# A pre-norm transformer layer on one core: GpSimd derives the norms' negated mean and variance plus epsilon, in place of VectorE

## What is computed

```python
x = x + attn(layernorm(x))     # 16 heads of 16, causal, window of 64 keys
x = x + ffn(layernorm(x))      # 256 -> 1024 -> 256, relu, ternary weights, biases

def layernorm(x, eps=1e-05):
    m = mean(x, axis=-1, keepdims=True)
    v = var(x, axis=-1, keepdims=True)
    return (x - m) / sqrt(v + eps)
```

## Time and profile before

| | before |
|---|---|
| median of the runs, us | 671.52 (667.95 to 671.65, 3 runs) |
| the profiled execution, us | 669.85 |
| its span, first to last instruction, us | 668.1 |
| mean granted TensorE clock | 0.992 |
| busy: PE, DVE, ACT, POOL, us | 645.6, 610.4, 565.0, 562.2 |
| instructions: PE, DVE, ACT, POOL | 8049, 1389, 2483, 837 |

### The profile page before, as it was taken

The page is one execution under the profiler, slowest core; times in us unless marked ns, Lnnn a source line. Parts: engine busy times, 40 slices in busy tenths (PEclk is TensorE's granted clock), DMA queues, the critical chain, the costliest instruction groups (busy, mean ns, idle before and its releaser), DMA issues.

```text
span 668.1 us, 23907 instructions
## 1 busy us (share of the span) xinstructions
PE 645.6 (97%) x8049; PEld 556.4 (83%) x8049; DVE 610.4 (91%) x1389; ACT 565.0 (85%) x2483; POOL 562.2 (84%) x837
## 2 busy tenths in 40 slices
PE   8787899999999999999999999999999999998998
PEld 5475778889888888888888888888888898888887
DVE  7899899999989999898999999899999989898975
ACT  6788899898889989888998989899898989788723
POOL 8899999888889898888889888888988889798831
PEclk9979999999999999999999999999999999999999
DMA  9454444454453545444354544544454353344110
GB/s 307 111 126 87 122 79 98 100 129 107 94 120 81 126 96 128 108 95 117 82 126 98 137 98 96 120 87 121 95 138 98 66 133 70 100 90 100 36 49 32
DMA packets 187025, 70.19 MB, mean 105 GB/s; under 512 B 155284, under 2 KB 178454, under 8 KB 186904
## 3 DMA queue, kind: packets, MB, share of 16 engines
q1 hardware_dynamic: 155816, 41.27, 30.0%
q10 hardware_dynamic: 31088, 27.40, 13.6%
HBM read 20.35 MB, written 9.44 MB: 45 GB/s over the span
## 4 chain that ended last, share of the span: by engine, by line
PE 80%; DVE 7%; SPq 4%; issue 2%; DMA 2%; POOL 2%; ACT 1%; ACTq 1%; DVEq 0%; POOLq 0%
PE ps L1261 16%; PE ps L1248 14%; PE ps L1155 12%; PE ps L1133 11%; PE ps L1194 10%; PE ps L1221 6%; PE ps L1207 5%; SPq L353 2%; PE ps L1233 2%; PE ps L1125 2%; PE ps L1181 2%; SPq L325 2%; DVE negm L835 2%; PE ps L1256 1%; DVE pt L852 1%
## 5 line engine op out<-in xcount | busy, mean ns | idle before, releaser
L632 ACT ACTIVATE p<-ps,negm 128x96 f32<-128x96 f32 x1024 | 336.4, 358 | 13.4 <-DVE negm L835 12.7
L503 POOL TENSOR_TENSOR tl<-pt,th 128x384 f16<-128x384 f32 x256 | 235.2, 919 | 20.7
L632 ACT ACTIVATION_READ_ACCUMULATOR p<-ps,negm 128x1 f32 x1024 | 230.2, 225 | 0.0
L835 DVE TENSOR_REDUCE negm<-ps 128x4 f32<-128x384 f32 x256 | 137.7, 538 | 27.7 <-PE ps L1133 25.1
L501 POOL CAST th<-pt 128x384 f16<-128x384 f32 x256 | 128.9, 504 | 25.6 <-DVE pt L852 24.9
L852 DVE STREAM_TRANSPOSE pt<-p 128x384 f32<-128x384 f32 x256 | 143.5, 561 | 2.4 <-ACT p L632 2.2
L1133 PE MATMUL ps<-k,qbd 128*128 128x96 f16 x1536 | 124.0, 207 | 0.0
L1133 PEld LDWEIGHTS ps<-k,qbd 128*128 128x128 f16 x1536 | 112.1, 113 | 9.7
L1155 PE MATMUL ps<-th,vb 128*128 128x96 f16 (+1 forms) x1120 | 100.3, 204 | 0.0
L1155 PE MATMUL ps<-tl,vb 128*128 128x96 f16 (+1 forms) x1120 | 100.3, 205 | 0.0
L1248 PE MATMUL ps<-xTCh,w1T 128*128 128x256 f16 x512 | 97.6, 272 | 0.0
(11 more groups left out here) (151 smaller groups left out, 1406.4 us busy)
## 6 DMA issues: line engine op xcount, KB each, us to landing
k<-kst SPq DMA_DIRECT2D x32, 288.0 KB, 3.8
rwide<-parked ACTq DMA_DIRECT2D x32, 256.0 KB
qbd<-qs SPq DMA_DIRECT2D x252, 32.0 KB, 2.5
vb<-vd SPq DMA_DIRECT2D x248, 32.0 KB, 2.0
out<-x ACTq DMA_DIRECT2D x31, 256.0 KB, 2.1
x<-in_L_attn_hidden ACTq DMA_DIRECT2D x15, 512.0 KB, 4.8
kw<-kst SPq DMA_DIRECT2D x30, 192.0 KB, 4.0
k<-kst SPq DMA_DIRECT2D x32, 144.0 KB, 3.5
```

The costliest lines, as they stand in the source:

```text
L503: e.tensor_tensor(tl[g % 2][:, o], pt[n % 3][:, :], th[g % 2][:, o], ALU.subtract).then_inc(s_lo, 1)
L632: ins = e.activation(p[:, 96 * u:96 * u + 96], bank[:, 96 * u:96 * u + 96], ACT.Exp, bias=m[:, u:u + 1], accum_out=r[:, u:u + 1])
L835: e.tensor_reduce(negm[n % 4][:, :], sbank[n % 3][:, 0:384].rearrange("p (a b) -> p a b", b=96), AX.X, ALU.max, negate=True).then_inc(s_mx, 1)
```

## The change

Both mvA and mvC lose the column with epsilon, and its two fills go. The two tensor_reduce behind each group of aggregates leave DVE, with the wait ahead of them. `rstd_a` and `rstd_c` on POOL now begin with a wait on the aggregates, a tensor_scalar that multiplies the mean by -1, one that adds 1e-5 to the variance, and the wait on the latter that was already there, now on POOL's own work. DVE's bn_stats gain a wait on the aggregates of the norm before. The results go where they went, and rows are still normalised with a scale and a shift.

```diff
@@ -185,8 +185,8 @@
         stA = sb("stA", [128, 4, 6], f32)
         stC = sb("stC", [128, 2, 6], f32)
 
-        mvA = sb("mvA", [128, 4, 3], f32)
-        mvC = sb("mvC", [128, 2, 3], f32)
+        mvA = sb("mvA", [128, 4, 2], f32)
+        mvC = sb("mvC", [128, 2, 2], f32)
         veA = sb("veA", [128, 4], f32)
         veC = sb("veC", [128, 2], f32)
         meanA = sb("meanA", [128, 4], f32)
@@ -447,6 +447,9 @@
 
             def rstd_a(c):
                 m = c % 2
+                e.wait_ge(s_agA, c + 1)
+                e.tensor_scalar(meanA[:, :], mvA[:, :, 0], -1.0, None, ALU.mult)
+                e.tensor_scalar(veA[:, :], mvA[:, :, 1], 1e-5, None, ALU.add).then_inc(s_mvA, 1)
                 e.wait_ge(s_mvA, c + 1)
                 if c >= 2:
                     e.wait_ge(s_xnA, 2 * c - 2)
@@ -456,6 +459,9 @@
 
             def rstd_c(h):
                 m = h % 2
+                e.wait_ge(s_agC, h + 1)
+                e.tensor_scalar(meanC[:, :], mvC[:, :, 0], -1.0, None, ALU.mult)
+                e.tensor_scalar(veC[:, :], mvC[:, :, 1], 1e-5, None, ALU.add).then_inc(s_mvC, 1)
                 e.wait_ge(s_mvC, h + 1)
                 if h >= 2:
                     e.wait_ge(s_xnC, h - 1)
@@ -775,10 +781,8 @@
         def _(e):
             def consts():
                 e.memset(mhalf[:, :], -0.5).then_inc(s_const, 1)
-                e.memset(mvA[:, :, 2:3], 1e-5)
                 e.memset(onesf[:, :], 1.0)
                 e.memset(ones[:, :], 1.0).then_inc(s_const, 1)
-                e.memset(mvC[:, :, 2:3], 1e-5)
                 for t in range(2):
                     e.memset(rden[t][:, :, 16:32], 0.0)
                 e.memset(qbd[1][:, :, :, :, :].rearrange("p g a j b -> p (g a j b)").bitcast(f32), 0.0).then_inc(s_zu, 1)
@@ -863,6 +867,8 @@
                 e.wait_ge(d_x[c % NX], 16 * (c // NX + 1))
                 if c == 0 and u:
                     e.wait_ge(d_xb, 16)
+                if c >= 1 and u == 0:
+                    e.wait_ge(s_agA, c)
                 for t in (2 * u, 2 * u + 1):
                     e.bn_stats(stA[:, t, :], xs[c % NX][:, t, :]).then_inc(s_stA, 1)
 
@@ -871,11 +877,8 @@
                 if c >= 1:
                     e.wait_ge(s_rsA, c)
                 for t in range(4):
-                    ins = e.bn_aggr(mvA[:, t, 0:2], stA[:, t, :])
+                    ins = e.bn_aggr(mvA[:, t, :], stA[:, t, :])
                 ins.then_inc(s_agA, 1)
-                e.wait_ge(s_agA, c + 1)
-                e.tensor_reduce(meanA[:, :], mvA[:, :, 0:1], AX.X, ALU.max, negate=True)
-                e.tensor_reduce(veA[:, :], mvA[:, :, 1:3], AX.X, ALU.add).then_inc(s_mvA, 1)
 
             def a_t(c, k):
                 w = 8 * c + k
@@ -941,17 +944,16 @@
             def c_stats(c, u):
                 h = 2 * c + u
                 e.wait_ge(s_cdv, USE[c, f"wo{u}"] + 1)
+                if h >= 1:
+                    e.wait_ge(s_agC, h)
                 for t in range(2):
                     e.bn_stats(stC[:, t, :], xs[c % NX][:, 2 * u + t, :]).then_inc(s_stC, 1)
                 e.wait_ge(s_stC, 2 * h + 2)
                 if h >= 1:
                     e.wait_ge(s_rsC, h)
                 for t in range(2):
-                    ins = e.bn_aggr(mvC[:, t, 0:2], stC[:, t, :])
+                    ins = e.bn_aggr(mvC[:, t, :], stC[:, t, :])
                 ins.then_inc(s_agC, 1)
-                e.wait_ge(s_agC, h + 1)
-                e.tensor_reduce(meanC[:, :], mvC[:, :, 0:1], AX.X, ALU.max, negate=True)
-                e.tensor_reduce(veC[:, :], mvC[:, :, 1:3], AX.X, ALU.add).then_inc(s_mvC, 1)
 
             def first_of_last():
                 h = 2 * NCH - 2
```

## The result

The kernel after takes 675.92 us in the median of 5 runs (673.53 to 676.86), against 671.52 (667.95 to 671.65) before: 1.0073 times as long, 95% interval 1.0044 to 1.0103. Against the 670.2 us and the 667.0 to 673.0 that I predicted, it is 5.7 us slower than predicted, and its fastest run lies above my range. The kernel before ran 75 more times beside the experiments, with a median of 669.64, so its own level of about 670 was not the mistake.

The account below looks back on a forecast made before the run. PE was taken to bound the steady part. Start -0.1, boundaries -0.5 and end +0.1 gave -0.5 us; between 669.35 and 671.0 us it predicted 670.2 us, no change, range 667.0 to 673.0.

Parts of the forecast that it names:

- the steady part: From 106 to 586 us: POOL's 39.7 us of waits absorb the 16 us needed, PE stays busy, effect 0.
- The threshold for POOL: POOL decides the steady part once a norm needs over 1.07 us more, operations costing more than about 0.5 us each.
- The price of an operation: Each small tensor_scalar on POOL takes 0.20 us, making a norm there 0.43 us longer (bounds 0.23 to 1.2).
- The end: Last chunk's first half: cover 0.05 us against 0.18 us of delay, so PE's transposes come late, +0.1 us.
- the second half's norm has more room ... and stays hidden: Last chunk's second half: the first half's feed-forward stands ahead of its transposes on PE, so its delay costs nothing.
- My upper bound there: Last chunk: at most +0.9 us, if an operation on POOL takes 0.57 us.
- The start: Up to about 80 us: DVE's relief against POOL's delays, -0.1 us (bounds -0.52 and +0.3).
- nearer the middle since the chain changes between the two: Early part: the chain alternates between DVE and POOL, so -0.1 was taken between -0.52 and +0.3 us.
- a rival, at a chance of 0.13 and 671.5 us: Early part: POOL's delays add and PE stays at 1.2 GHz longer, +0.9 to +1.8 us; chance 0.13.
- The boundaries: Two later chunk boundaries: PE's waits for the keys each shorten by DVE's 0.26 us through SyncE's queue, -0.5 us.
- POOL as the bound: Steady part: dearer small operations use up POOL's slack, 675.5 or 708 us; chance 0.04, of which 0.03 over 1%.
- 667.4: Start and chunk boundaries: PE's waits for the keys vanish, -3.3 us in place of -0.5; chance 0.15.

Follow-up runs that it names:

- double: The kernel after with two more spare small tensor_scalar on POOL ahead of each norm's own, and a wait on them: 689.67 us, 1.0281 of before.
- end: The kernel before with the operations moved to POOL only for the last six norms C: median 671.77 us, 1.0031 of before.
- start: The kernel before with the operations moved only for the first four norms A and first two norms C: median 672.18 us, 1.0036 of before.
- mid: The kernel before with the operations moved only for the 36 norms of the steady part: median 670.05 us, 1.0002 of before.
- start_a: The kernel before with the operations moved only for the first four norms A: 670.65 us, 1.0011 of before.

## Why the prediction was wrong

**The bottleneck and the steady part were right.** PE stayed busy for all of 106 to 586 us, POOL took the added work out of its waits, and moving 36 norms there changed the time by 0.02%. The threshold for POOL was bracketed by double. DVE's busy time came out at 599.7 (near 596 said) and POOL's at 584.7 (near 580 said).

**The price of an operation was 0.24, not 0.20,** and the distance from one start to the next is 0.30 where I had 0.15 for the second one, by taking the overlap of 0.05 us that POOL shows between long instructions. With 0.65 instead of 0.43 us a norm, nothing changes in the steady part, but the two ends scale with it.

**The end: +0.1 said, +1.4 measured.** The step that failed is "the second half's norm has more room ... and stays hidden", together with looking at the last chunk alone. The last stretch grew by 1.36 us (1.40 in end). PE waits for 1.06 us at h 29, whose cover of 0.06 us stands in the trace as plainly as h 30's, 15 us earlier, and for 0.40 at h 30. I had weighed a norm's latency against its own cover, but behind POOL's last idle time each norm's occupancy adds to the next. At h 30 the power came 0.37 us later and not 0.18: the two operations end behind one another before it may start, 0.70 us from the aggregates' end to the power (649.71 to 650.41 us) against 0.33. My upper bound there was 0.9.

**The start: -0.1 said, about +1.3 and then a lower clock measured.** From the first score mask to the first transposes it is 64.42 us in after, 64.87 in start, and 62.76 to 63.37 in the four kernels with nothing moved there. The step that failed is the choice "nearer the middle since the chain changes between the two". After the change the chain no longer changes: from 24.6 to 84.9 us it runs through POOL alone. Its last pieces (start, length, piece):

```profile
80.97 0.93 POOL tl L509
81.90 0.08 issue
81.99 0.24 POOL meanC L463
82.23 0.06 issue
82.29 0.24 POOL veC L464
82.53 0.07 issue
82.60 0.73 POOL rstdC L468
...
83.71 1.14 POOL xnC L497 x2
84.85 0.04 issue
84.90 0.82 PE ps L1235 x4
...
86.57 2.40 PE ps L1209 x12
```

Three norms stand on it (A of chunks 2 and 3, and the first C), and DVE's 0.26 us of relief at each is worth nothing once DVE is no longer on the chain. 3 x 0.65 us less the idle time of 0.29 and 0.30 us that POOL had there before is 1.36 us, an estimate that fits. The first norm C is in no term of my prediction, which counted the two norms A only. The last row is the second part: twelve matmuls in 2.40 us that take 1.31 at the full clock. I had that as a rival, at a chance of 0.13 and 671.5 us, and its mechanism is the one that came in the profile of after. I had put it before 69 us, where PE is idle anyway, and not behind the first xnC, where PE already waited for 1.49 us in the kernel before. That wait stands in none of my rows.

**The boundaries: -0.5 said, nothing seen.** The keys' waits were 3.3 us in three before and 5.4 in two after, and the stretch that holds the later one took 37.3 to 41.8 us in the profiled kernels, in no relation to what was moved (mid 40.21, start_a 37.77). The 0.35 us that after gains between the first bias matmul and the one near 580 is the wait of 0.34 us at 266 us, which after doesn't have; but start_a and end, with nothing moved there, don't have it either. The step that failed is a gain of 0.26 us through a queue whose own scatter is many times that.

**The sum.** Counted again with what was measured: start about +1.3, lower clock +1.4 in the executions that have it, end +1.4, boundaries unknown: +4.1 us. Added to before's 669.64 that is 673.7; by the median measured beside after (671.52) it is 675.6; measured were 675.92. The rest, up to 2 us, I can't assign; the wait for keys near 614 us and the lower clock behind it can be part of it. The means at equal clock tell the same: at a mean granted clock of 0.990 after takes 674.74 us (3 runs) and before 671.42 (14 runs), +3.3 us; and after's mean clock over its runs is 0.988 against 0.992. The part that hangs on the clock is seen in few profiles and is argued from them and from these means, not shown run by run, and the means can't tell the stretch behind the first xnC from the one near 617 us.

**The range** had two faults. Its upper end took the slow start (671.5) with some scatter, but not the slow start together with its bounds at the end (+0.9), and both come from the same cause, a longer POOL. And the chance of slower by over 1% was sized on POOL as the bound alone. The rivals' times don't share a base either: 675.5 is the profiled execution's 669.85 with 5 and 0.9 added, while 667.4 and 671.5 start from 670.7 and 670.2.

## What to carry to other kernels

Slack of an engine over a long stretch says nothing on the two ends: for each, find the last idle time on the engine that gets the work, and from there on add its occupancy at every place up to the consumer, not only the latency at the tightest one. List all consumers of what that engine produces whose cover is below the price of the change (here two, at 633 and 648 us, and one with a wait of 1.49 us that was already there). A wait that grows on TensorE can cost more than its length, through the clock in the microseconds behind it.

## What the runs showed of the hardware

- **A subtraction in GpSimd's tensor_scalar** more than doubles its time: 1250 and 1253 ns against 574 (multiply, add) and 568 (add, multiply) for 128 x 255 in float32. Adding a negated operand is the cheap form. A negation of 128 x 2 or 128 x 4 by multiplying with -1 takes 238 to 243 ns.
- **A small tensor_scalar on GpSimd hardly depends on its size:** 219 to 238 ns for 2 elements a row and 233 to 243 for 4, 0.30 us from start to start, so they follow each other with a gap and don't overlap as the long ones do.
- **The same wait of TensorE is sometimes followed by 1.2 GHz and sometimes not:** 2.09 us and a clock of 1.00 behind it, 2.10 us and 0.79, in two executions of one kernel. The Trainium skill (TensorE: Matmul & The Clock Gate, Part 1) says that the gate doesn't start with the kernel, and that the same code therefore changes level at different places from run to run; these two executions agree with it, and no run here shows the gate's own phase.
- **The scatter of a kernel's runs follows the mean granted clock:** before takes 668.63 us at 0.995 (17 runs), 669.86 at 0.992 (34), 671.42 at 0.990 (14) and 673.64 at 0.987 (4). One step of 0.0025 is 0.005 x 668 = 3.3 us at the lower level, of which half, an estimated 1.7 us, is lost; the means grow by 1.2 to 2.2 us a step. The waits that go with the lower level are in these times too.
